# Causal attention in an attention-and-FFN kernel: heads of a group on two halves of the PE's rows

## The reference

```python
# x (4, 1024, 128) f32, 16 heads of 8, causal attention
qkv = x @ W_qkv.T + b_qkv                     # reshaped to (b, t, 3, 16, 8)
scores = jnp.einsum('bhqd,bhkd->bhqk', Q, K) / np.sqrt(8)
attn = jax.nn.softmax(scores + causal, axis=-1)
x = _layernorm(x + (einsum('bhqk,bhkd->bhqd', attn, V) @ W_o.T + b_o))
# then: a gated MLP (128 -> 512 -> 128) plus, for each token and each of 4 heads, the 8 best
# of 64 x 64 product keys, whose experts are weighted by a softmax of their scores
x = _layernorm(x + ffn(x))
```

## Time and profile before

| | |
|---|---|
| median of three runs | 861.89 us (860.15 to 862.83) |
| the profiled execution | 859.2 us, of which its span is 857.6 us |
| busy over the span | PE 86%, DVE 80%, ACT 66%, POOL 49% |
| first stage | 0 to about 61 us |
| attention | about 62 to 550 us |
| mean granted PE clock | 0.94 |

### The profile page before, as it was taken

How to read it: one execution, slowest core, us unless ns; L and a number is a source line. 1 busy time by engine, 2 the same in 40 slices (tenths; PEclk the granted TensorE clock), 3 DMA queues, 4 the chain that set the end, 5 groups by cost and what they waited for, 6 DMA issues and landing times. The chain is left out here.

```text
span 857.6 us, 17568 instructions
## 1 busy us (share of the span) xinstructions
PE 739.3 (86%) x4345; PEld 323.0 (38%) x4345; DVE 683.2 (80%) x2289; ACT 567.2 (66%) x926; POOL 423.4 (49%) x468
## 2 busy tenths in 40 slices
PE   6758999999999999999999998696788888887755
PEld 4432233333332333233323331243456555554345
DVE  5669999898988898898889881156788888888883
ACT  4440267666766676667666767558889797897881
POOL 8655112221222112211222122267899999999984
PEclk9875699999999999999999999987999999999997
DMA  6757535335533653364336331201001101100000
GB/s 174 226 152 198 114 71 132 76 93 116 128 76 84 125 120 75 81 137 116 86 74 137 82 68 33 90 2 52 1 0 38 38 1 37 38 1 13 1 14 25
DMA packets 58955, 67.06 MB, mean 78 GB/s; under 512 B 15488, under 2 KB 33536, under 8 KB 58880
## 3 DMA queue, kind: packets, MB, share of 16 engines
q1 hardware_dynamic: 53120, 62.35, 30.5%
q10 hardware_dynamic: 5184, 2.36, 1.0%
q0 software_dynamic: 576, 1.57, 0.7%
HBM read 46.73 MB, written 19.53 MB: 77 GB/s over the span
## 5 line engine op out<-in xcount | busy, mean ns | idle before, releaser
L697 ACT ACTIVATE probs<-ps 128x384 f32<-128x384 f32 (+2 forms) x384 | 291.9, 810 | 174.4 <-PE ps L751 123.4
L668 POOL TENSOR_SCALAR_AFFINE_SELECT probs<-probs 128x256 f32<-128x256 f32 x256 | 102.9, 407 | 368.6 <-ACT probs L697 366.3
L807 DVE CUSTOM_DVE_ANT_0 junk<-ps,tri 128x256 bf16<-128x256 f32 (+3 forms) x512 | 229.1, 488 | 43.7 <-PE ps L719 36.0
L719 PE MATMUL ps<-Kx,Qx 128*128 128x512 bf16 (+3 forms) x768 | 230.8, 345 | 11.3 <-DVE mx L811 4.1
L751 PE MATMUL ps<-Qa,Ka 128*128 128x512 bf16 (+3 forms) x768 | 185.9, 328 | 15.0 <-DMA Qa<-m_scr 10.1
L737 PE MATMUL ps<-probs,Vg 128*9 128x512 f32 (+3 forms) x1536 | 159.3, 488 | 1.0 <-ACT Os L682 0.5
L811 DVE TENSOR_REDUCE mx<-ps 128x1 f32<-128x512 f32 x256 | 158.2, 679 | 0.3 <-DVE Vg L794 0.2
L719 PEld LDWEIGHTS ps<-Kx,Qx 128*128 128x128 bf16 x768 | 68.7, 97 | 204.4 <-DVE mx L807 124.8
L966 POOL TENSOR_TENSOR S<-sim 128x1024 f32<-128x1024 f32 x64 | 120.6, 1907 | 12.1 <-DVE A L1218 6.5
L1218 DVE SCALAR_TENSOR_TENSOR A<-S,T,ps 128x511 f32<-128x511 f32 x128 | 90.2, 741 | 11.3 <-ACT ps L1040 10.3
L751 PEld LDWEIGHTS ps<-Qa,Ka 128*128 128x128 bf16 x768 | 61.5, 97 | 90.8 <-ACT probs L697 44.3
(11 more groups left out here) (115 smaller groups left out, 868.5 us busy)
## 6 DMA issues: line engine op xcount, KB each, us to landing
Qx<-q_scr SPq DMA_DIRECT2D x48, 192.0 KB
Kx<-k_scr SPq DMA_DIRECT2D x48, 192.0 KB
Qa<-q_scr SPq DMA_DIRECT2D x48, 192.0 KB
Ka<-k_scr SPq DMA_DIRECT2D x48, 192.0 KB
o_scr<-Os SPq DMA_DIRECT2D x32, 256.0 KB, 2.1
q_scr<-qs SPq DMA_DIRECT2D x34, 128.0 KB, 3.3
k_scr<-qs SPq DMA_DIRECT2D x18, 128.0 KB, 3.3
xin<-in_L_attn_x_dram ACTq DMA_DIRECT2D x8, 256.0 KB, 3.7
```

Source lines behind the costliest of these rows:

```text
L668: pool.affine_select(out=diag, in_=diag, compare_op=ALU.is_ge, fill=0.0, base=0, pattern=[[0, 2], [1, P]], channel_multiplier=-1).then_inc ...
L697: act.activation(probs[:, k % 2, hh, 0:width], ps[:, bank:bank + 2, :].rearrange("p a c -> p (a c)")[:, 0:width], ACT.Exp, scale=SM_SCALE) ...
L719: pe.matmul(ps[:, X_BANK + f % X_SLOTS, 0:c1 - c0], Qx[:, u, hh, P * i:P * (i + 1)], Kx[:, u, hh, c0:c1], start=True, stop=True).then_inc( ...
L807: dve.tensor_tensor_reduce(out=junk[:, f % 4, 0:w], in0=src, in1=tri[:, CHUNK - w:CHUNK], scale=1.0, scalar=-BIG, op0=ALU.add, op1=ALU.max ...
```

## The change

Four heads of a group are held in `PL` = 2 planes by two halves: half `a` has 64 rows of the tiles (`ROWS`), and every operand tile has 2 planes of 1024 tokens instead of 4 heads of 1024. Of the nine terms eight stand in the 64 rows. The maximum is taken from these eight. The scores take the ninth term and the maximum's three rows from new tiles `Ql`/`Kl` in a second matmul that adds to the first. So a chunk of the maximum is one matmul of 64 rows, with two heads on the two halves in succession and in different banks, and a step of the scores is now two heads of one key tile: four matmuls. There are still 24 steps and 24 calls of ACT, of the same number of columns in all. The masks are of two heads of one tile instead of two tiles of one head, 16 as before. `probs` has four slots of one key tile. The order string, `AHEAD` (17) and the places of ACT's copies (steps 13 and 8 instead of 12 and 4) and of DVE's copy of V (chunk 40 instead of 12) are others. The loads and the order on SP change, and `m_rows` is four stores and two loads instead of one store and four loads. The first stage has four slots of `qs`, its loops are written out, SP stores 4 tiles a chunk instead of 6, and the bias loads and the first copy of weights put the columns into the new order.

```diff
-AHEAD = 20
-GROUP_ORDER = "psxxxpxxsxxsxsxpxspxxsxxpxxxspxxssxxsxpxsxxxsxpxxxsxspsxxsxpxxsxsxxsxpxxsxpxsxsxsxsx"
+PROB_SLOTS = 4
+AHEAD = 17
+GROUP_ORDER = "pxsxsxxpxxxsxxsxpxsxsxpxsxxsxxssxpxxxppxsxxsxpxxsxxxsxxxsppxsxxsxsxxxsxspxssxxpsxxsx"
-COPY_AT = (12, 4)
+COPY_AT = (13, 8)
+VG_AT = 40
+QS = 4
+X_LOADS, S_LOADS, M_LOADS = 10, 14, 2
...
+        Qx, Kx, Qa, Ka, Ql, Kl = [operands.enter_context(nc.sbuf_tensor(name, [P, 2, PL, SEQ], BF16))
+                                  for name in ("Qx", "Kx", "Qa", "Ka", "Ql", "Kl")]
...
         def load_parts(eng, qdst, kdst, g, done):
+            for a in range(2):
+                q, k = [dst[ROWS * a:ROWS * (a + 1)].rearrange("p j t -> p (j t)") for dst in (qdst, kdst)]
+                qsrc = q_scr[g, a].rearrange("n s d j t -> (n s d) (j t)")
+                eng.dma_start(q[0:2 * FULL], qsrc.unsqueeze(0).broadcast_to([2, FULL, PL * SEQ])).then_inc(done, 16)
+                eng.dma_start(q[2 * FULL:ROWS], qsrc[0:ROWS - 2 * FULL]).then_inc(done, 16)
+                for s in range(PARTS):
+                    ksrc = k_scr[g, a, s].rearrange("n d j t -> (n d) (j t)")
+                    times = PARTS if s < PARTS - 1 else PARTS - 1
+                    eng.dma_start(k[FULL * s:FULL * s + DH * times], ksrc.unsqueeze(0).broadcast_to(
+                        [times, DH, PL * SEQ])).then_inc(done, 16)
+
+        def load_last(eng, u, g, done):
+            for a in range(2):
+                for dst, scr in ((Ql, q_scr), (Kl, k_scr)):
+                    eng.dma_start(dst[ROWS * a + PARTS:ROWS * a + PARTS + DH, u, :, :].rearrange("p j t -> p (j t)"),
+                                  scr[g, a, PARTS - 1].rearrange("n d j t -> (n d) (j t)")).then_inc(done, 16)
...
-                            act.wait_ge(qk_stored[u], STORES * 16 * b + ONE)
+                            if b > 1:
+                                act.wait_ge(qk_stored[n % QS], STORES * 16)
...
                     def group(n, u, ahead):
                         sp.wait_ge(s_ready, SPG * n + ONE)
                         load_parts(sp, Qa[:, 1 - u], Ka[:, 1 - u], bass.ds(n + 1, 1), sop_loaded[1 - u])
-                        store_o(n, 0)
+                        load_last(sp, 1 - u, bass.ds(n + 1, 1), sop_loaded[1 - u])
+                        if not isinstance(n, int) or n > 0:
+                            store_o(n - 1, 1)
+                        m_rows(n + 1, 1 - u, bass.ds(n + 1, 1))
                         if ahead:
                             load_next_max(n + 3, 1 - u)
-                        m_rows(n + 1, 1 - u, bass.ds(n + 1, 1))
-                        store_o(n, 1)
+                        store_o(n, 0)
...
-                    pool.memset(Qa[:], 0.0).then_inc(pads_made, 1)
-                    pool.memset(Ka[:], 1.0).then_inc(pads_made, 1)
...
-                            if hh == 0:
-                                act.wait_ge(pv_done, PPG * n + 2 * (k - 1) + PV_START)
+                            if pl == 0:
+                                act.wait_ge(pv_done, PPG * n + t - PROB_SLOTS + 1 + PV_START)
...
-                        pe.matmul(ps[:, X_BANK + f % X_SLOTS, 0:c1 - c0], Qx[:, u, hh, P * i:P * (i + 1)],
-                                  Kx[:, u, hh, c0:c1], start=True, stop=True).then_inc(mx_ready, 1)
+                        a, pl = divmod(hh, PL)
+                        rows = slice(ROWS * a, ROWS * (a + 1))
+                        pe.matmul(ps[:, X_BANK + f % X_SLOTS, 0:c1 - c0], Qx[rows, u, pl, P * i:P * (i + 1)],
+                                  Kx[rows, u, pl, c0:c1], start=True, stop=True).then_inc(mx_ready, 1)
...
-                        for j, q0, w, off in UNITS[k][1]:
-                            bank = S_BANK + 2 * (e % 2) + off // CHUNK
-                            mm = pe.matmul(ps[:, bank, off % CHUNK:off % CHUNK + w], Ka[:, u, hh, P * j:P * (j + 1)],
-                                           Qa[:, u, hh, q0:q0 + w], start=True, stop=True)
+                        for q, k, first in ((Qa, Ka, True), (Ql, Kl, False)):
+                            for a in range(2):
+                                rows = slice(ROWS * a, ROWS * (a + 1))
+                                mm = pe.matmul(ps[:, S_BANK + 2 * (e % 2) + a, 0:w], k[rows, u, pl, P * j:P * (j + 1)],
+                                               q[rows, u, pl, q0:q0 + w], start=first, stop=not first)
```

More of the change, by code:

```diff
@@ L24 @@
 PARTS = 3
-SPLIT_ROWS = PARTS * PARTS * DH
-M_ROW = SPLIT_ROWS
+PL = GH // 2
+ROWS = P // 2
+FULL = PARTS * DH
 VW = DH + 1
@@ L39 @@
 FAR = 1.0e38
[L43 to L46, removed]
+KTILES = []
+for _half in range(2):
+    for _j in range(4 * _half + 4):
         _q0 = max(P * _j, CHUNK * _half)
[L48 to L59, removed]
+        KTILES.append((_half, _j, _q0, CHUNK * (_half + 1) - _q0))
+PPG = len(KTILES)
+HALF_PIECES = sum(_half == 0 for _half, _j, _q0, _w in KTILES)
+DIAG_TILES = [t for t, (_half, _j, _q0, _w) in enumerate(KTILES) if _j >= 4 * _half]
+SPG = PPG * PL
+MPG = len(DIAG_TILES) * PL
+PROB_SLOTS = 4
 MAXC = []
@@ L203, in build @@
         p3_made = sem("p3_made")
-        qk_stored = [sem(f"qk_stored{u}") for u in range(2)]
-        p3_stored = [sem(f"p3_stored{u}") for u in range(2)]
+        qk_stored = [sem(f"qk_stored{u}") for u in range(QS)]
+        p3_stored = [sem(f"p3_stored{u}") for u in range(QS)]
         pads_made = sem("pads_made")
@@ L341, in _ @@
                 def _(sp):
-                    for signal in (*qk_stored, v_ready, p3_made, s_ready, *o_stored, o_read):
+                    for signal in (s_ready, *o_stored, o_read):
                         sp.sem_inc(signal, ONE)
@@ L361, in _ @@
                                  allow_slow_non_contiguous=True).then_inc(wts_loaded, 16)
-                    with sp.Fori(0, BATCH - 1) as b:
+                    for b in range(BATCH - 1):
                         store_parts(sp, b)
                     for u in range(2):
-                        sp.wait_ge(qk_stored[u], STORES * 16 + ONE)
+                        sp.wait_ge(qk_stored[u], STORES * 16)
                         sp.wait_ge(p3_stored[u], 32)
-                    sp.wait_ge(pads_made, 2)
                     load_parts(sp, Qx[:, 0], Kx[:, 0], bass.ds(0, 1), xop_loaded[0])
@@ L490, in _ @@
                     turn(0, 0)
-                    with pe.Fori(0, BATCH - 1) as b:
+                    for b in range(BATCH - 1):
                         turn(b, 1)
@@ L556, in _ @@
                     copy_turned(0, 1)
-                    with dve.Fori(0, BATCH - 1) as b:
+                    for b in range(BATCH - 1):
                         for u in range(2):
@@ L635, in _ @@
                     group(GROUPS - 2, 0, False)
+                    store_o(GROUPS - 2, 1)
                     for half in range(2):
@@ L840, in group @@
                         for f in range(CPG):
-                            if f == 12 and last < 2:
+                            if f == VG_AT and last < 2:
                                 dve.wait_ge(pv_done, PPG * n + PV_START)
```

211 lines of the change are left out of this document (106 added, 105 removed).

## The result

The changed kernel takes 1011.76 us (median of 4 runs, 1009.55 to 1013.98), the kernel before beside it 862.36 (860.15 to 862.99). The ratio is 1.174, 95% interval 1.170 to 1.177: 149 us slower, where 820 us, 42 us faster, was forecast. The profiled execution has a span of 1010.8 us against 857.6.

The account below looks back on a forecast made before the run. The prediction took DVE and PE, holding each other up, as the bound, with DVE left after the change. From 859.2 us it took 35.6 (steady groups), 2 (last groups) and 4.5 (first stage): 817, median 820; range 804 to 835.

Parts of the forecast that it names:

- The bytes are about the same, and the DMA share is 0.45.: SP's loads in the attention: the prediction's remark on their traffic, with no time added for them.
- with over a group of slack: SP's loads for the maximum two groups on, behind the rows' store: claimed to have over a group's time to spare.
- a new wait for DMA in front of the first step of a group: Attention: one of the listed signs that would show the forecast wrong; no size given.
- The rows' order: SP: the maxima's store goes ahead of the Qx and Kx loads, so PE's wait goes, worth 1.1 us a group.
- Period: Attention's steady groups: 28.64 us each falls to 26.1, near DVE's floor, bounds 25.1 and 27.5; 35.6 us over 14 groups.
- The halves work at the same time: PE's row halves overlap: the maximum streams 3.5 us less a group (bounds 0 to 3.9), scores cost +0.3.
- an overhead of the added matmuls: PE, maximum: a counterargument that 48 added matmuls at 25 ns would cost an estimated 1.2 us a group.
- Rival 2: PE's halves do not overlap: 34 to 35 us a group, PE-bound, 940 us; chance 0.12 together with rival 3.
- the first stage: Before the attention: four slots end ACT's store waits, chunks 5.0 us apart instead of 5.8, 5.7 us gained, net 4.5.
- The last groups: From the last transpose to the attention's end, 35.1 us: a gain of 2 us, bounds 0 to 4.
- rival 3: PE's clock falls because PE streams less: 39 us a group at 1.2 GHz, above 950 us; chance 0.12 together with Rival 2.
- ACT's waits for `k_scr`: First stage: 17.9 us of ACT waits in 6 places for stores of the chunk two before, forecast to go.

Follow-up runs that it names:

- e11: e2_copies with only the maximum's tiles Qx and Kx loaded as in the change, copies outermost: 881.32 us, ratio 1.024 to the kernel before.
- e4: The kernel before with one edit, the maximum's rows ahead of the Qx and Kx loads on SP: 865.36 us, ratio 1.007.
- e9: e4 with all loops of the attention written out: 844.30 us, ratio 0.981 to the kernel before.
- e10: The kernel before with nothing but the attention's loops written out on all five engines: 851.17 us, ratio 0.990.
- e7: e6_cyclic with DVE's loop over pairs of groups alone written out: 821.12 us, ratio 0.954 to the kernel before.
- e15: e7 with all matmuls of the maximum and scores reading the first half of the rows only: 946.04 us, ratio 1.099 to the kernel before.
- e6_cyclic: e2_copies with the terms in another order of rows, so 16 loads do for a pair of tiles instead of 22: 843.94 us, ratio 0.983 to the kernel before.
- e2_copies: The changed kernel with each copy of Q's and K's parts a DMA of its own, 22 loads instead of 10: 845.68 us, ratio 0.984 to the kernel before.

## Why the prediction was wrong

**The step that failed** is in the part on SP: "The bytes are about the same, and the DMA share is 0.45." The loads were costed at nothing by bytes and by a mean share. But a load's time goes by how many of its packets can be in flight: 12.6 before, with 24 rows outermost, and 2.0 after, with 2 or 3 copies outermost. It cost 166 us: 1011.8 against 845.7 with the same bytes in loads of another form. The sentence before it fell with it, "with over a group of slack": e11 shows PE waiting for these very tiles. The wait that the prediction named as a sign against it, "a new wait for DMA in front of the first step of a group", is what the trace shows; no rival carried it.

**A second term was mis-sized**, and hid a cost: with the loads mended the kernel takes 844, not 820. The rows' order was priced at 28.64 - 27.54 = 1.1 us a group, from the one group without the wait. The 27.5 is right for a group without a jump: 27.63 in e4, 27.52 in e9. But that group is the one in which DVE's loop ends and doesn't jump back, so the difference holds two things. With all loops written out the wait alone is 28.26 - 27.52 = 0.7 us a group (e10, e9), 7 us in all. The rest is the jump, of which the sum has no term: in every second group it stood partly under the wait for the rows, and cost 9 us even so. Once that wait is gone, DVE's loop costs 844 - 821 = 23 us, of which 17 are in its six jumps.

**The terms that held**, with loads mended and DVE's loop written out (e7):

- Period 26.22 us for 26.1, so 33.9 us for 35.6. Some 5 of the 33.9 are not the change's: the period before was 28.64 with loops and 28.26 without (e10).
- The halves work at the same time. In the changed kernel score matmuls of the two halves start 5 ns apart (302.033 and 302.038). The 1.2 us a group that the prediction worked out as an overhead of the added matmuls don't show either: e15, in which PE is the bound, takes 33.5 us, with 31 of streaming and 3 to 5 for changes of tiles by the prediction's own terms. Rival 2 is e15: 946 us for 940 (its own terms, 862 + 83 + 10 less 4.5 for the first stage, come to 950).
- The last groups gained 1.3 of 2 us: 33.2 us from e7's last transpose to its last product, before 34.5.
- The clock (rival 3) did fall to 0.86 on average, but PE's idle time came first. In the changed kernel PE waits 6.76 us for the rows before its matmul at 417.29 us, and within that wait the clock goes from 1.00 to its lower level, 1.2 GHz. In e7 it is 1.00 in the whole steady part, with less streamed than before.

```profile
412.00:413.50 1.50, 0.00 (x0) 0.00 (x0) 0.69 (x1) 0.00 (x0) 0.00 (x0) 1.00 0.14 52
413.50:415.80 2.30, 0.00 (x0) 0.00 (x0) 0.00 (x0) 0.00 (x0) 0.00 (x0) 0.51 0.02 3
415.80:420.40 4.60, 3.11 (x19) 0.88 (x19) 1.42 (x3) 1.78 (x2) 0.41 (x1) 0.50 0.19 44
```

- In the first stage ACT's waits for `k_scr` are gone. Its first and last chunk in the changed kernel:

```profile
14.56 0.69 ACT L461 ACTIVATE qf<-ps,bqk 128x512 f32<-128x512 f32 x1 [1.19 <-PE ps L495]
...
43.56 0.69 ACT L461 ACTIVATE qf<-ps,bqk 128x512 f32<-128x512 f32 x1 [0.51 <-PE ps L495]
```

They are 29.0 us apart instead of 40.7: chunks 4.1 us apart, not the 5.0 taken. Only 5.5 of these 11.7 us reach the second transpose of e7 (108.22 against 113.68); the others become a wait for the first load of Kx, which the forecast had no term for. PE's first matmul of the attention starts at 56.26 us in e7 after a wait of 6.69 us for it, and at 61.81 in the kernel before after 1.09 us of another wait. That 4.5 was forecast is so in part luck. In the changed kernel this matmul starts at 66.19, after 16.39 us: the slow loads took the gain and more.

The sum of e7, 33.9 + 5.5 + 1.3 = 40.7 us, less 2 us lost behind the attention, gives its 38.5 in spans (857.6 to 819.1), for 42 forecast. So the overlap and DVE's bound were read rightly; the transfers that feed them weren't looked at as transfers. That e7 lands at 821, beside the forecast of 820, is partly luck, since it needs an edit that the forecast didn't have: with the loads mended alone the change gains 15 or 16 us (0.983 and 0.984), not 42.

**Left open:** why e11's later waits for Kx come mostly in the turns of the loop, and what fills the 2.4 of the 2.8 us of DVE's jump in which the trace has no transfer of instructions.

## What to carry to other kernels

When an edit changes the access pattern of a DMA, count it by packets per engine: the outermost dimension on either side, the packets that fall on the busiest engine, and their time from the trace; the mean DMA share says nothing of it, and a small transfer lands late behind loads that keep to few engines (9.5 us here instead of 1.1). Before taking a gain from the one undisturbed group, ask what differs between it and the others apart from the wait named. And look, at a loop's end, for idle time put down to issue: writing the loops out gave 9 us to a kernel that seemed tuned, and DVE's alone gave 23 to the better one.

## What the runs showed of the hardware

- Only DVE's jump is dear. Branch to next instruction took 2.8 to 4.2 us on average on DVE (over five kernels), and 0.28 on PE and 0.15 on ACT (e6_cyclic). Between two branches the trace of e6_cyclic has 354 instructions on DVE, 1132 on PE (weight loads and matmuls both counted) and 67 on ACT, so the length of the body alone does not say which jump is dear. The Trainium skill, "Runtime: NRT & Kernel Launch", section "Instruction fetch mechanics", says that a taken branch whose target isn't in the engine's buffer of two pages of 256 instructions (PE's holds 2048 in all) waits for a DMA of the target, and that unrolling is preferred. That sorts the three as seen: 354 back may lie outside, 67 is inside, and so is 1132 on PE. No run here varied the length of DVE's body (354 in the kernel before too), so that this is the reason is not shown.
- Issue time goes with the form too: 0.30 us for a load of 24 rows outermost, 0.64 to 0.85 for one with 2 or 3 copies outermost.
- An untouched transfer suffers with them: the store of O landed in 12.4 us instead of 2.1, and in 2.3 again in e2_copies (medians of 32).
- Score matmuls on the two halves of the rows started 3 to 5 ns apart in the closest quarter of the pairs (e7); on one half 55 ns was the least (e15).
